# Eight more weight halves split by GpSimd during the first top-k search, and three edits to that top-k, in a four-sequence transformer block on one Trainium2 core

## Reference

```python
# layer 0: mask of the 5120 largest entries of a 512 x 512 matrix
adj = (emb_s * emb_t) * (softmax(x, axis=-1) / sqrt(512))
adj[diag] = -inf
x = x + mask_of_top_k(adj, k=5120)              # 1.0 at the 5120 largest
# layer 1: D = 512, H = 16 heads of DH = 128, MLP width 2048
shift1, scale1, gate1, shift2, scale2, gate2 = split(cond @ ada_w + ada_b, 6)
x1 = ln(x) * (1 + scale1) + shift1
q, k, v = split(x1 @ qkv_w + qkv_b)             # 3 x 16 heads
y = softmax(q @ k.T / sqrt(DH)) @ v @ out_w + out_b
z = x + gate1 * y
x2 = ln(z) * (1 + scale2) + shift2
out = x + z + gate2 * (gelu(x2 @ ffn_w1 + b1) @ ffn_w2 + b2)
```

## Time and profile before

| | |
|---|---|
| median of 3 runs | 1718.7 us (1718.33 to 1719.66) |
| profiled execution | 1722.43 us, span 1720.7 us |
| PE busy / PEld busy | 1621.3 us (94%) / 1356.1 us (79%) |
| DVE / ACT / POOL busy | 1181.7 us (69%) / 863.5 us (50%) / 142.3 us (8%) |
| first matmul of sequence 0 after the top-k | 121.5 us from the start |
| mlp_in of sequence 0 begins | 426.48 us |

### The profile page before, as it was taken

One profiled execution on the slowest core, in us unless ns is written; L12 is line 12 of the kernel. 1 busy time (PEld: TensorE's weight loads), 2 busy tenths in 40 slices (PEclk: granted clock), 3 DMA queues, 4 the chain that ended last, 5 costly groups with the idle time before them and its releaser, 6 DMA issues.

```text
span 1720.7 us, 22533 instructions
## 1 busy us (share of the span) xinstructions
PE 1621.3 (94%) x8268; PEld 1356.1 (79%) x8268; DVE 1181.7 (69%) x2548; ACT 863.5 (50%) x1630; POOL 142.3 (8%) x81
## 2 busy tenths in 40 slices
PE   0759999999899999999999999999999999999998
PEld 0757888888777888888878888888878888888887
DVE  6776877767885887776775787776676576665321
ACT  3546566655753555554571555554472455444240
POOL 4002312213340000000000000000000000000000
PEclk9999999999999999999999999999999999999999
DMA  7023434437566332134454332323344431332453
GB/s 300 1 104 114 165 125 178 155 109 281 195 247 231 117 123 100 72 123 147 147 195 175 150 123 76 121 105 140 137 181 181 161 123 50 122 123 75 171 196 122
DMA packets 62702, 247.94 MB, mean 144 GB/s; under 512 B 4224, under 2 KB 4352, under 8 KB 60672
## 3 DMA queue, kind: packets, MB, share of 16 engines
q1 hardware_dynamic: 62592, 246.50, 38.7%
HBM read 191.95 MB, written 54.53 MB: 143 GB/s over the span
## 4 chain that ended last, share of the span: by engine, by line
PE 81%; DVE 12%; ACT 3%; issue 1%; DVEq 1%; DMA 0%; SPq 0%; ACTq 0%
PE bank L1053 23%; PE bank L1055 23%; PE bank L1054 23%; PE bank L1147 7%; DVE tb L738 3%; DVE cand L795 1%; DVE act L932 1%; DVE prob L908 1%; PE bank L1215 1%; PE bank L1210 1%; PE bank L1173 1%; PE bank L1077 1%; ACT prob L619 1%; PE bank L1211 1%; PE bank L1095 1%
## 5 line engine op out<-in xcount | busy, mean ns | idle before, releaser
L1053 PE MATMUL bank<-xT,w 128*128 128x512 f32 x704 | 279.8, 397 | 0.5 <-POOL w L468 0.5
L619 ACT ACTIVATE prob<-bank,nbias 128x512 f32<-128x512 f32 x256 | 176.6, 690 | 202.2 <-DVE nbias L905 202.2
L1055 PE MATMUL bank<-xT,w 128*128 128x512 f32 x704 | 274.2, 389 | 0.0
L1054 PE MATMUL bank<-xT,w 128*128 128x512 f32 x704 | 274.1, 389 | 0.0
L1053 PE MATMUL bank<-act,w 128*128 128x512 f32 (+1 forms) x576 | 218.2, 379 | 0.8 <-DVE act L869 0.8
L1055 PE MATMUL bank<-act,w 128*128 128x512 f32 (+1 forms) x576 | 211.6, 367 | 0.0
L1054 PE MATMUL bank<-act,w 128*128 128x512 f32 (+1 forms) x576 | 211.5, 367 | 0.0
L916 DVE TENSOR_TENSOR probT<-bank,probT 128x512 fp32r<-128x512 f32 x256 | 158.8, 681 | 24.8 <-ACT probT L629 24.5
L899 DVE TENSOR_REDUCE rowmax<-bank 128x1 f32<-128x512 f32 x256 | 174.6, 682 | 0.0
L1055 PEld LDWEIGHTS bank<-xT,w 128*128 128x128 f32 x704 | 132.2, 188 | 27.7
L1053 PEld LDWEIGHTS bank<-xT,w 128*128 128x128 f32 x704 | 132.1, 188 | 25.9 <-POOL w L468 0.9
(11 more groups left out here) (131 smaller groups left out, 3040.6 us busy)
## 6 DMA issues: line engine op xcount, KB each, us to landing
w<-split_weights SPq DMA_DIRECT2D x144, 1024.0 KB, 5.3
split_weights<-w SPq DMA_DIRECT2D x48, 1024.0 KB, 6.1
wraw<-weights_in SPq DMA_DIRECT2D x48, 512.0 KB, 3.9
adaw<-ada_w_in SPq DMA_DIRECT2D x4, 1536.0 KB, 14.7
xr<-x_in SPq DMA_DIRECT2D x4, 1024.0 KB, 7.4
out<-x SPq DMA_DIRECT2D x4, 1024.0 KB, 4.4
adj<-x_in SPq DMA_DIRECT2D x3, 1024.0 KB, 6.9
adj<-x_in SPq DMA_DIRECT2D x4, 256.0 KB, 4.4
```

Of the source, the lines that this page charges most:

```text
L619: nc.scalar.activation(prob[:, i, :], bank[i][:, :], ACT.Exp, bias=nbias[:, i:i + 1], scale=SCALE, accum_out=rowsum[:, i:i + 1]).then_inc( ...
L1053: pe.matmul(dst, w_hi_ap, x_hi_ap, start=first, stop=False)
L1054: pe.matmul(dst, w_hi_ap, x_lo_ap, start=False, stop=False)
L1055: return pe.matmul(dst, w_lo_ap, x_hi_ap, start=False, stop=last)
```

## The change

It has three parts. **First,** after the four early halves POOL rounds and splits eight more (`PRE`) during the first search: the two of the second value group (`v_half(1, 0)` and `v_half(1, 1)`) and the six of units 9, 10 and 11. They are not put into `w` but into one of two desks (`desk(k)`), which are the two halves of tile `xT`, idle until the first layernorm; SP stores them from there to `split_weights`, and later in sequence 0 loads them into their places as it does in the other sequences (`load_ahead`). ACT rounds nothing for them. A new list `ORDER` gives the order of raw loads and splits; `w_ready` and `w_hi` count along it, and PE waits for the eight by `w_in`. ACT waits for both desks to be stored before it writes `xT`. **Second,** in the top-k: the move of `cand` becomes a `tensor_scalar` with `step_up` as its scalar in place of a `scalar_tensor_tensor`; and `topk_mask` works on all four tiles in one instruction each, then makes the statistics by `row_stats`. `xm_ready` counts 1 for a sequence and not 4. **Third,** at the start: `small` and `tb` are loaded by ACT's queue, ahead of its work, and not by SP's; the exponential's table is loaded at once, and ACT waits for `small` only after the four exponentials.

```diff
+PRE = tuple([v_half(1, 0), v_half(1, 1)] + [unit_half(u, j) for u in (9, 10, 11) for j in range(2)])
+EARLY = 4
+ORDER = [n for n in range(EARLY)] + list(PRE) + [n for n in range(EARLY, NHALF) if n not in PRE]
+AT = {n: k for k, n in enumerate(ORDER)}
+AHEAD = EARLY + len(PRE)
+DESKS = 2
...
+        def desk(k):
+            at = (k - EARLY) % DESKS * 2 * HALF
+            return xT[:, :, :, :].rearrange("p a c t -> p (a c t)")[:, at:at + 2 * HALF]\
+                .rearrange("p (s n) -> p s n", s=2)
...
+            def load_ahead(n, freed, count):
+                wait_apart(sp, freed, count)
+                sp.wait_ge(w_saved[PLACE[n]], 16 * before_in_place(n, ORDER[:EARLY] + ORDER[AHEAD:]))
+                sp.dma_start(w_place(n), scratch[n]).then_inc(w_in[PLACE[n]], 16)
...
             def first_sequence():
-                load_raw(2, EARLY)
-                wait_apart(sp, xm_ready, NT)
+                load_raw(2, AHEAD + 2)
+                wait_apart(sp, xm_ready, 1)
                 load_x(1)
-                load_raw(EARLY, NQKV + 6)
+                for i in range(DESKS):
+                    sp.wait_ge(desk_saved[i], 16 * len(range(i, len(PRE), DESKS)))
+                for n in PRE:
+                    if n in (v_half(1, 0), v_half(1, 1)):
+                        load_ahead(n, v_done, QUAD)
+                load_raw(AHEAD + 2, AT[unit_half(3, 0)])
                 wait_apart(sp, pt_done, H * NT)
                 load_x_again(1)
-                load_raw(NQKV + 6, NHALF)
+                load_raw(AT[unit_half(3, 0)], NHALF)
                 save_split(NHALF - 2)
                 save_split(NHALF - 1)
+                for n in PRE:
+                    if n in (unit_half(9, 0), unit_half(9, 1)):
+                        load_ahead(n, f_done, KC)
+                    elif n in (unit_half(10, 0), unit_half(10, 1)):
+                        load_ahead(n, y2_done, Y2_CREDIT + 1)
+                    elif n in (unit_half(11, 0), unit_half(11, 1)):
+                        load_ahead(n, y2_done, Y2_CREDIT + 2)
...
+            def split_on_desk(k):
+                turn = (k - EARLY) // DESKS
+                if turn:
+                    pool.wait_ge(desk_saved[(k - EARLY) % DESKS], 16 * turn)
+                pool.wait_ge(raw_in[k % 2], 16 * (k // 2 + 1))
+                nc.gpsimd.tensor_copy(desk(k)[:, 0, :], wraw[:, k % 2, :]).then_inc(w_hi, 1)
+                pool.wait_ge(w_hi, k + 1)
+                nc.gpsimd.tensor_tensor(desk(k)[:, 1, :], wraw[:, k % 2, :], desk(k)[:, 0, :].bitcast(F32),
+                                        ALU.subtract).then_inc(w_ready, 1)
...
-            for n in range(EARLY):
-                split_early(n)
+            for k in range(EARLY):
+                split_early(k)
+            for k in range(EARLY, AHEAD):
+                split_on_desk(k)
             finish_modulation()
...
-            act_e.wait_ge(small_in, 16)
-            act_e.wait_ge(consts_ready, 3)
-            topk_exp(0)
+            act_e.dma_start(small[:, :], cols).then_inc(small_in, 16)
+            act_e.dma_start(tb[:, :], cond[0:1, :].to_broadcast([P, T])).then_inc(tb_in, 16)
+            act_e.wait_ge(consts_ready, 3)
+            nc.scalar.activation(table[:, :], ident[:, 0:1], ACT.Exp)
+            topk_exp(0)
+            act_e.wait_ge(small_in, 16)
...
-                move = V.scalar_tensor_tensor(cand[:, :], step_up[:, :], -bit / 2, cand[:, :], ALU.add, ALU.add)
+                move = V.tensor_scalar(cand[:, :], cand[:, :], step_up[:, :], -bit / 2, ALU.add, ALU.add)
...
-                for i in range(NT):
-                    part = slice(i * T, (i + 1) * T)
-                    V.scalar_tensor_tensor(eqm[:, part], rank[:, part], need[:, :], low[:, part],
-                                           ALU.subtract, ALU.is_le)
-                    dve.drain()
-                    V.tensor_tensor(xm[:, i, :], xr[:, i, :], eqm[:, part], ALU.add).then_inc(xm_ready, 1)
-                    dve.drain()
-                    V.bn_stats(stats[:, i, 0, :], xm[:, i, :])
+                V.scalar_tensor_tensor(eqm[:, :], rank, need[:, :], low[:, :], ALU.subtract, ALU.is_le)
+                dve.drain()
+                V.tensor_tensor(xm[:, :, :].rearrange("p i d -> p (i d)"),
+                                xr[:, :, :].rearrange("p i d -> p (i d)"), eqm[:, :], ALU.add)\
+                    .then_inc(xm_ready, 1)
+                dve.drain()
```

More of the change, by code:

```diff
@@ L99 @@
 ADA_STEP = 8
-EARLY = 4
 FAR = float(1 << 20)
@@ L151, with before_in_place @@
 TURN, USES = turns()
+PRE = tuple([v_half(1, 0), v_half(1, 1)] + [unit_half(u, j) for u in (9, 10, 11) for j in range(2)])
[4 more added lines that the diff above has]
+DESKS = 2
+def before_in_place(n, among):
+    return sum(m in among for m in range(n) if PLACE[m] == PLACE[n])
 def is_first(b):
@@ L305, in wait_apart, with w_credit @@
             eng.sem_inc(waits_met, 1)
+        desk_saved = [sem(f"desk_saved{i}") for i in range(DESKS)]
+        def desk(k):
+            at = (k - EARLY) % DESKS * 2 * HALF
+            return xT[:, :, :, :].rearrange("p a c t -> p (a c t)")[:, at:at + 2 * HALF]\
+                .rearrange("p (s n) -> p s n", s=2)
+        def w_credit(place):
+            return USES[place] - sum(PLACE[n] == place for n in PRE)
         def w_place(n):
@@ L312, in w_wait @@
         def w_wait(eng, b, n):
-            if is_first(b):
-                eng.wait_ge(w_ready, n + 1)
+            if is_first(b) and n in PRE:
+                eng.wait_ge(w_in[PLACE[n]], 16 * (w_credit(PLACE[n]) + before_in_place(n, PRE) + 1))
+            elif is_first(b):
+                eng.wait_ge(w_ready, AT[n] + 1)
             else:
@@ L321, in _, with save_split @@
         def _(sp):
-            def save_split(n):
-                sp.wait_ge(w_ready, n + 1)
-                sp.dma_start(scratch[n], w_place(n)).then_inc(w_saved[PLACE[n]], 16)
-            def load_raw(lo, hi):
[L328 to L333, removed]
+            def save_split(k):
+                n = ORDER[k]
+                sp.wait_ge(w_ready, k + 1)
+                if n in PRE:
+                    sp.dma_start(scratch[n], desk(k).bitcast(F32)).then_inc(desk_saved[(k - EARLY) % DESKS], 16)
+                else:
+                    sp.dma_start(scratch[n], w_place(n)).then_inc(w_saved[PLACE[n]], 16)
+            def load_raw(lo, hi):
+                for k in range(lo, hi):
+                    if k >= 2:
+                        sp.wait_ge(w_ready, k - 1)
+                    sp.dma_start(wraw[:, k % 2, :], weights[ORDER[k]]).then_inc(raw_in[k % 2], 16)
+                    if k >= 2:
+                        save_split(k - 2)
+            def load_ahead(n, freed, count):
+                wait_apart(sp, freed, count)
+                sp.wait_ge(w_saved[PLACE[n]], 16 * before_in_place(n, ORDER[:EARLY] + ORDER[AHEAD:]))
+                sp.dma_start(w_place(n), scratch[n]).then_inc(w_in[PLACE[n]], 16)
             def load_split(b, n, freed, count):
@@ L426, in _ @@
             for place in PLACES:
-                sp.sem_inc(w_in[place], 16 * USES[place])
+                sp.sem_inc(w_in[place], 16 * w_credit(place))
             for i in range(NT):
                 sp.dma_start(rank[:, i * T:(i + 1) * T], x_seq[0][:, i * T:(i + 1) * T]).then_inc(x0_in[i], 16)
-            sp.dma_start(tb[:, :], cond[0:1, :].to_broadcast([P, T])).then_inc(tb_in, 16)
-            sp.dma_start(small[:, :], cols).then_inc(small_in, 16)
             load_raw(0, 2)
@@ L553, in split_hi @@
             def split_hi(b, n, freed, count):
-                if not is_first(b) or n < EARLY:
+                if not is_first(b) or AT[n] < AHEAD:
                     return
@@ L558, in split_hi @@
                 act_e.wait_ge(freed, count)
+                k = AT[n]
                 if TURN[n]:
-                    act_e.wait_ge(w_saved[PLACE[n]], 16 * TURN[n])
-                act_e.wait_ge(raw_in[n % 2], 16 * (n // 2 + 1))
-                nc.scalar.copy(w[:, region, 0, half * HALF:(half + 1) * HALF], wraw[:, n % 2, :])\
+                    act_e.wait_ge(w_saved[PLACE[n]], 16 * before_in_place(n, ORDER[:EARLY] + ORDER[AHEAD:]))
+                act_e.wait_ge(raw_in[k % 2], 16 * (k // 2 + 1))
+                nc.scalar.copy(w[:, region, 0, half * HALF:(half + 1) * HALF], wraw[:, k % 2, :])\
                     .then_inc(w_hi, 1)
@@ L722, in _ @@
             act_e.wait_ge(ada_ready, 1)
+            for i in range(DESKS):
+                act_e.wait_ge(desk_saved[i], 16 * len(range(i, len(PRE), DESKS)))
             ln_hi(0, ada1[:, 0:C], ada1[:, C:2 * C])
@@ L1019, in sequence @@
                             topk_mask(b + 1)
+                            row_stats(xm, 0, 0, D)
                             normalise(b * LNS + LNS, xm, 1)
```

30 lines of the change are left out of this document (15 added, 15 removed).

## The result

The changed kernel takes 1706.69 us (median of 6 runs, 1704.24 to 1708.25), the kernel before 1719.18 in the same session; the ratio is 0.9917, 95% interval [0.9906, 0.9928] (the ratio on record; the quotient of the two medians is 0.9927). It is faster, as forecast, by 12.5 us in the medians and by 14.2 in the profiled executions (spans 1720.7 and 1706.5), where 19.2 were forecast. The median lies 0.7 us above the top of the forecast range, 1706; that range starts from 1718.7 us for the kernel before, and the ratio applied to 1718.7 gives 1704.4, inside it.

A forecast was written before the change was run, and what follows sets the result against it. PE was taken to bound the kernel, except DVE before the first value tile, with POOL holding the engine PE waited for. Eight terms summed to −19.2 us: 1718.7 to 1699.5, range 1692 to 1706.

The forecast's parts named there:

- the contention itself: DVE instructions with two SBUF tensors, or wide tensor_scalar, are held until POOL's instruction ends; a one-column tensor_scalar is not.
- the lower level: After search step 16: two DVE instructions may each be held by POOL's desk work, +2.2 us (nothing to 4.7).
- the mask: First mask, L823 to L838: one-piece instructions take 7.4 us for 9.0, −1.6; nothing in the other three masks.
- the start: Kernel start: exponentials no longer wait for `small`, so L761 starts earlier, −2.3 us (0.6 to 3.4).
- the slots of mlp_in: mlp_in and first unit of mlp_out: two held moves go, one held by a unit 9 subtraction; −2.0 us (1.0 to 4).
- Head 0: Sequence 0: PE's 2.36 us wait goes with ACT's roundings and POOL's hold, and the half clock behind it; −4.1 us.
- If the new move behaves like L905 all of it goes: −6.3: First search's 32 steps: stretched moves (5.8 us) and a count 0.5 late vanish; eight more halves add nothing.
- first rival: The move is held all the same, its scalar being read from SBUF: 1718.3 us, no change; 6%.
- Gone with their cause: −4.6: Rest of mlp_out: without units 10 and 11's four subtractions, PE's 2.9 us gate wait and the half clock after it go.
- the out projection: Its first search step is held by a subtraction that stays; with the new move PE's 0.6 gate wait shrinks, −0.5 (0 to 0.9).
- Rest: 84% for the forecast, range 1693 to 1705: start, lower level, mlp_in, and a 1.7 us half-clock stretch may vary.

The follow-up runs named there:

- x1: Changed kernel with the old move of cand (scalar_tensor_tensor, two SBUF tensors), twelve halves on POOL: 1715.8 us, ratio 0.9961.
- x9: Changed kernel with only the two value halves on desks, and the first search's step in PSUM, read there by the old move form: 1704.36 us, ratio 0.9898.
- x11: x8 with the first search's step in PSUM, read there by the old move form: 1702.39 us, ratio 0.9889.
- x8: Changed kernel with POOL held back ahead of its fourth desk half until the lower level is built: 1703.63 us, ratio 0.9901.
- x2: Changed kernel without desks: the eight halves rounded by ACT and split by POOL in sequence 0 as before: 1707.58 us, ratio 0.9917.
- x5: Kernel before with the new move of cand alone: 1715.08 us, ratio 0.9969.
- x7: Changed kernel with ACT copying a raw half at the two places of head 0 where it rounded before, POOL idle there: 1704.12 us, one run.
- x6: Kernel before with the mask in one piece alone: 1715.14 us, ratio 0.9969.

## Why the prediction was right, and where it was not

The direction was right. Of the 19.2 us forecast, three quarters came in the profiled executions (14.2) and two thirds in the medians (12.5).

*Right with its mechanism and size:* the contention itself (x1, x9, x11); the lower level, +2.1 for +2.2, with x8 as the proof that it was POOL; the mask, −1.6; the start, −2.0 for −2.3; the slots of mlp_in, −2.2 for −2.0, though the move alone gives it, without unit 9 (x2, x5). The Trainium skill ("SBUF — State Buffer", Who interferes with whom) says that a DVE instruction with two SBUF inputs contends with a GpSimd instruction that reads SBUF. The runs agree: over the steps up to 54 us, with POOL at work, the move takes 0.88 us on average with two SBUF tensors (x1) and 0.158 with one of them in PSUM (x9).

*Head 0,* −3.6 for −4.1: the desks did it (x2), for the larger part by taking away POOL's subtraction and for the smaller by taking away ACT's rounding (x2 against x7). Most of the missing 0.5 is the slow first matmuls, 0.4.

*The step that failed in size* is "If the new move behaves like L905 all of it goes: −6.3". L905 has an immediate as its scalar and takes 0.15 us; the new move reads its scalar from SBUF and takes 0.214. None of the moves was held, but each of the 32 pays 0.055 over the old form undisturbed, 1.8 us together, and the held count (0.5) stayed; it is a delay of issue that is there with every form of the move. So the 32 steps gave −4.0 and not −6.3. The prediction saw the difference of form in its first rival, but only as a reason why the move might be held.

*The step that failed in its cause* is "Gone with their cause: −4.6" in the rest of mlp_out. The gain came (−5.0), but the removed subtractions were not needed for it. With them in place and the mask in one piece it is as large (x2, x6); with the old mask and the new move it is missing (x5). Before, four holds of 1.8 to 2.1 us fell on the narrow instructions and z, some 8 us; in x2 three are left, 1.8, 2.0 and 2.2, and the mask is 1.6 shorter, so DVE is 3.7 us earlier at the gate, and the wait there was 2.9. The prediction counted the mask's form for nothing in sequence 0's mlp_out because DVE "lies under PE"; that was so in sequences 1 and 2, and not in the one where PE waited for it. By the same rows, taking away the four subtractions alone would remove 8 us of holds, which is more than 2.9 as well; that is an estimate, since the desks were not run with the old mask. Either part then removes the same wait, and that the size came out right is luck in part: the forecast gave it to one part and nothing to the other.

*Missing term:* a half-clock stretch in sequence 1, +1.6, which only x9 of the other kernels shows, though all of them have the wait in front of it; the range allowed for it, the sum did not. With the 1.8 of the move's scalar it makes up 3.4 of the 5 us between −19.2 and −14.2. Sequence 2 is 0.5 longer; it is 0.2 to 0.5 longer than before in every kernel run here, and that was not looked into. *Mis-sized:* the out projection, −0.1 for −0.5: the move is free there, but the same subtraction now holds L869 (4.33 us, as L804 before), and the gate's wait stays 0.6. *The range:* the single ranges under *Rest* add up to 1694.2 and 1706.4, not 1693 and 1705.

*Open:* what decides whether half clock follows a wait of 1.7 us (in sequence 1 it does in 2 of the 14 kernels profiled, the changed one and x9), and why the first matmuls of the value tiles stay slow longer in the same two (0.7 and 0.9 us).

## What to carry to other kernels

Before work is moved to GpSimd, list what VectorE does beside it by operands: in these runs an instruction with two SBUF tensors, however short, and a wide `tensor_scalar` waited until GpSimd's ended, while the count with its accumulator did not. A one-column move in a serial search pays all that is left of GpSimd's instruction. Make such instructions few and wide, or give them one operand in PSUM, before buying relief by moving the other side: here the new move and the one-piece mask gave what six of the eight moved halves were credited with. And undo the parts one at a time, in both directions: when two parts remove the same wait, either looks like its cause.

## What the runs showed of the hardware that was not expected

- A `tensor_scalar` of one column with its scalar read from SBUF takes 0.214 us, one with an immediate 0.15 (L905); a `scalar_tensor_tensor` takes 0.158, with a tensor in PSUM too.
- The hold goes both ways, as far as one row shows it: POOL's subtraction takes 3.20 us and not 2.35 when L866 runs as it starts.
- Half clock for 3.4 us came after each of the six waits of PE of 2.0 to 3.0 us (before, x2, x5, x6), and after two of the 28 waits of 1.7 us that the 14 profiles have in sequences 1 and 2.
